# Softmax denominators of the graph units: inverted on 16 columns and spread by small transfers instead of VectorE transposes

## The chip, the cores and the metric

The kernel runs on one core of one Trainium2 chip. The metric is the time of one execution on the device, in microseconds (us); three runs of the kernel before took 3496.37, 3509.16 and 3542.75 us, so its median is 3509.16 us.

## The reference, cut to what matters

A sequence model of two layers. The first is an attention layer with 8 heads over 4 sequences of 1024 tokens of 128 numbers. The second is a graph of six nodes, each of them an attention layer without mask over the same tokens, whose query, key and value come from earlier nodes:

```python
for c in range(6):
    nsrc = min(c + 1, 5); snode = c - nsrc
    q = ew[c, 0] * (nodes[c - 1] @ We[eq] + be[eq])
    k = ew[c, 1] * (nodes[snode] @ We[ek] + be[ek])
    v = ew[c, 2] * (nodes[snode + nsrc // 2] @ We[ev] + be[ev])
    # mha: heads of 16; scores = qh @ kh.T / 4; attn = softmax(scores); ctx = attn @ vh; ctx @ Wo[c]
    nodes[c] = act_w[c] * mha(q, k, v, Wq[c], Wk[c], Wv[c], Wo[c]) + q
```

At the end stand a layer norm and the residual. Everything is float32. The change lies in the division by the softmax's sum, in the graph alone.

## The kernel before, in words

The graph (function `graph`) has 24 **units**, one for each node and sequence, in a fixed order; unit u + 4 reads what unit u stored in DRAM. A unit has 8 heads in two halves of 4 (`QUAD`), and 2 chunks of 512 queries. That makes 4 **groups** of a unit (`NG`; first both chunks of the first half, then both of the second) and 96 in the graph. Group g of the graph is group g % 4 of unit g // 4; "the unit's last group" is its fourth.

A unit is written as 46 **rounds** (the last unit, which prepares nothing for another, has 64). In a round PE makes the transposed scores of one head for 128 keys by 512 queries twice into one pair of PSUM banks (`pair`), and once more into the bank `psX` (a single). ACT takes the exponential of the pair in one instruction (L1454) and of the single in another (L1460). There is one pair bank, so the next round's pair waits for the exponential of this one. Some rounds use `psX` for something else: the next unit's values and projections, the transposed maxima (`turn`), or the unit's output. A table by the round's number sets this (`V_ROUND`, `PJ_ROUND`, `TURN_ROUND`, `OUT_ROUND`).

**Maxima.** The softmax needs each query's maximum beforehand. For the next unit PE computes all scores once more in 64 pieces of 128x1024 (`maxima`, L1262) into two PSUM buffers, and DVE reduces each piece (L1491). Piece p waits until piece p - 2 is reduced (`mx_done`). The pieces are spread over the rounds, about 1.4 a round.

**Contexts and denominators.** `contexts` multiplies the exponentials with the values of 4 heads at once, each head in a slot of 32 PSUM partitions: 16 rows of context and 16 equal rows of the sum of exponentials, since half the value columns are ones. When a group's 8 blocks of keys are done, ACT copies the 128x512 result to SBUF (`c_b`, L1439). Then DVE inverts the denominators in three steps, one in each of the three rounds after the copy, between reductions: a transpose of 32x32 blocks (`den_b`, L393), a reciprocal of the one column in 32 that holds a sum and a copy that spreads it over 16 columns (L403, L405), and a transpose back (`rec_b`, L414). GpSimd multiplies (`normalise`, L1552 and L1555), and for the second half adds the first (L1557). PE turns the chunk's context into the output (L1336, L1337), ACT copies it (`nt_b`, L1433), and SP stores it in DRAM.

**What sets the order.** Each engine's instructions are a list written out in Python; it executes them in that order and waits on semaphores. SP issues all transfers of the graph, and its list for a unit (`unit` in the block of SyncE) is: the second half of the stacked queries and keys of unit u + 1 (`stack`, 12 transfers `qs_`/`ks_<-partd`), the loads for its values and for the projection of unit u + 2 (`xq`, `xk`, `xv`), the rows of maxima (`maxima_rows`, 4 transfers `qs<-mpart` of 8 KB), the previous unit's second store, the residual's loads, the spill of unit u + 2 (`partd<-part`, 2 MB) and the first half of its stack, the next unit's rows of maxima, and the first store. On SP a wait for a semaphore keeps everything behind it waiting.

In the traces `_b` marks tiles of the graph, `ps_max` the maxima's buffers, `ps_pair` the pair bank, `ps_misc` psX.

Of the kernel before, what the change touches and what calls it, by code (L numbers as in the profile page):

```python
# [100 lines left out]
def program(nc, x, w_qk, w_v, w_out, b_out, conv, conv_rev, ew, act_w, We, be, Wq, Wk, Wv, Wo, ln_g, ln_b,  # L101
            ident, exchange, out):
    def dram(name, shape):
        return nc.dram_tensor(name, shape, F32, kind="Internal").ap()

    xnt = dram("xnt", [BATCH, P, TOK])
    x1d = dram("x1d", [BATCH * NCHUNK, P, BPC, DIM])
    node = dram("node", [UNITS + BATCH, P, TOK])
    ext = dram("ext", [4, HEADS, NE])
    wpd = dram("wpd", [NODES, P, WP_COLS])  # L110
    wvd = dram("wvd", [NODES, P, P])
    wfd = dram("wfd", [NODES, P, WF_COLS])
    partd = dram("partd", [P, 2, 2, TOK])
    x_rows = x.rearrange("b (t p) d -> b p t d", p=P)
    out_rows = out.rearrange("b (t p) d -> b p t d", p=P)

    with ExitStack() as ctx:
        def psum(name, n):
            return ctx.enter_context(nc.psum_tensor(name, [P, n], F32))

        psM = [psum(f"ps_max{i}", TOK) for i in range(2)]
        psP = psum("ps_pair", 2 * CHUNK)
        psS = [psP[:, CHUNK * i:CHUNK * i + CHUNK] for i in range(2)]
        psO = psum("ps_ctx", CHUNK)
        psX = psum("ps_misc", CHUNK)
        sid = ctx.enter_context(nc.sbuf_tensor("ident_sb", [P, P], F32))
# [8 lines left out]
        graph(nc, psM, psP, psO, psX, sid, wpd, wvd, wfd, node, partd, stored)  # L135
        finish(nc, psM, sid, node, x1d, ln_g, ln_b, out_rows)


# [859 lines left out]
    return slice(i, i + 1) if isinstance(i, int) else bass.ds(i, 1)  # L998


def graph(nc, psM, psP, psO, psX, sid, wpd, wvd, wfd, node, partd, stored):

    with ExitStack() as ctx:
# [14 lines left out]
        c32, rec = sb("c32_b", [P, 2, CHUNK]), sb("rec_b", [P, CHUNK])  # L1020
        den, inv = sb("den_b", [P, CHUNK]), sb("inv_b", [P, CHUNK // SLOT])
# [17 lines left out]
        o_copied, den_step, rec_ready, cn_done = sem("b_o_copied"), sem("b_den_step"), sem("b_rec_ready"), sem("b_cn_done")  # L1039
        fin_ready, fin_copied = sem("b_fin_ready"), sem("b_fin_copied")  # L1040

        PJ = 2 * NCHUNK
# [2 lines left out]
        NG = 2 * NCHUNK  # L1045
        STACK = 4 * len(TERMS) * D16
        MROWS = 4 * D16
        AHEAD = PIECES + 4
        LAST = UNITS - 1

        V_ROUND = {9: 0, 12: 1}
        PJ_ROUND = {14: 0, 18: 1, 20: 2, 23: 3}
        TURN_ROUND = ({33: 0, 16: 1}, {26: 0, 1: 1})
        OUT_ROUND = ({42: 0, 7: 1}, {58: 0, 10: 1})

        def single(u, r):

            turn = TURN_ROUND[u > 0].get(r)
            if turn == 1:
                return "turn", u, 1  # L1060
            if turn == 0 and u < LAST:
                return "turn", u + 1, 0
            out = OUT_ROUND[u == LAST].get(r)
            if out is not None and u >= out:
                return "output", u - out, out
# [65 lines left out]
        with nc.Block() as block:  # L1131
            @block.sync
            def _(sp):
# [47 lines left out]
                def maxima_rows(w, q):  # L1181
                    sp.wait_ge(mp_done, 2 * w + q + 1)
                    for k in range(2):
                        for odd in range(2):
# [45 lines left out]
                stack(1, 0)  # L1230
                for u in range(UNITS):
                    unit(u)
                store(LAST, 1)
                sp.wait_ge(stored, (UNITS + BATCH) * NCHUNK * D16)

# [251 lines left out]
            def _(dve):  # L1487
# [13 lines left out]
                def inverses(at):  # L1501

                    for step in range(1, 4):
                        g = GROUP_ROUND.get(at - step)
                        if g is None:
                            continue
                        if step == 1:
                            denominators_turned(nc, dve, c32, den, g, g % 2, o_copied, den_step, ones)
                        elif step == 2:
                            denominators_inverted(nc, dve, den, inv, wide, g // 2 % 2, g, cn_done, den_step)  # L1510
                        else:
                            inverses_turned(nc, dve, rec, wide, g // 2 % 2, g, rec_ready, den_step, ones)

                def unit(u):
                    for r in range(ROUNDS[u]):
                        for w, p in pieces_at(u, r, 0):
                            maxima(w, p)
                        inverses(sum(ROUNDS[:u]) + r)
                        for w, p in pieces_at(u, r, 1):
                            maxima(w, p)  # L1520

                nc.vector.memset(neg[:], -1.0).then_inc(minus, 1)
                for i in range(2):
                    nc.vector.memset(wide[i][:], 0.0)
                    for q in range(2):
                        ins = nc.vector.memset(vs[i][:, :, QUAD * q:QUAD * q + QUAD, DV * (1 - q):DV * (2 - q)], 1.0)
                ins.then_inc(ones, 1)
# [3 lines left out]
                    maxima(0, p)  # L1531
                for u in range(UNITS):
                    unit(u)
                g = NG * UNITS - 1
                denominators_turned(nc, dve, c32, den, g, 1, o_copied, den_step, ones)
                denominators_inverted(nc, dve, den, inv, wide, 1, g, cn_done, den_step)
                inverses_turned(nc, dve, rec, wide, 1, g, rec_ready, den_step, ones)

            @block.gpsimd
            def _(pool):  # L1540
# [3 lines left out]
                    nc.gpsimd.tensor_tensor(mpart[:, 1], m32[:], mpart[:, 0].bitcast(F32), ALU.subtract).then_inc(mp_done, 1)  # L1544

                def normalise(u, g):
                    pool.wait_ge(rec_ready, NG * u + g + 1)
                    if u:
                        pool.wait_ge(fin_ready, NCHUNK * (u - 1) + g % 2 + 1)
                    c = g % 2  # L1550
                    if g < 2:
                        nc.gpsimd.tensor_tensor(cn[:, 0, c], c32[:, c], rec[:], ALU.mult).then_inc(cn_done, 1)  # L1552
                        return

                    nc.gpsimd.tensor_tensor(cn[:, 1, c], c32[:, c], rec[:], ALU.mult).then_inc(cn_alone, 1)  # L1555
# [149 lines left out]
```

## Time and profile before

| | |
|---|---|
| median of three runs | 3509.16 us |
| profiled execution | 3483.55 us |
| its span, first to last instruction | 3481.7 us |
| TensorE busy (matmul) | 3058.8 us, 88% |
| VectorE busy | 2517.9 us, 72% |
| ScalarE busy | 2290.9 us, 66% |
| GpSimd busy | 489.1 us, 14% |
| mean granted TensorE clock | 0.953 of 2.4 GHz |

The preparation and the first attention layer take the first 950 us, the graph runs from there to about 3435 us, and the final layer norm ends the program. Busy shares are averages over these stages. "PEld" is the loading of weights into TensorE, "SPq" the issue of transfers on SP; an idle time in square brackets is what an engine stood idle just before an instruction, and behind the arrow is what released it. A transfer's time to landing runs from its issue to the semaphore.

### The profile page before, as it was taken

How to read it: one execution, taken by the hardware profiler on the slowest of the kernel's cores; microseconds unless marked ns; L12 is line 12 of the kernel's file. 1: busy time of each engine (PE TensorE's matmuls, PEld its weight loads, DVE VectorE, ACT ScalarE, POOL GpSimd, SP SyncE). 2: the span in 40 equal slices, each digit the busy share in tenths (PEclk: the TensorE clock that was granted, in tenths of full speed). 3: DMA queues.
4: the chain of work that ended last, by engine and by line, in shares of the span. 5: the costliest groups of instructions: out<-in, count | busy, mean ns of one | idle time of the engine just before them, and what ended most of it. 6: DMA issues, size and time to landing. Idle time of an engine off the chain costs nothing. (4 is left out here: it accounts for less than half of the span.)

```text
span 3481.7 us, 46771 instructions
## 1 busy us (share of the span) xinstructions
PE 3058.8 (88%) x17215; PEld 1373.0 (39%) x17215; DVE 2517.9 (72%) x2916; ACT 2290.9 (66%) x3238; POOL 489.1 (14%) x392
## 2 busy tenths in 40 slices
PE   5699998999758999999999999999999999999994
PEld 4466665656413333333333333333333333333331
DVE  5756554555248888888888788878888888888853
ACT  1355665655515677777777677777777777777783
POOL 0211101111000011111111111111111111111103
PEclk9899999999858999999999899999999999999996
DMA  5000000000144343344334433433444334433402
GB/s 162 16 10 4 23 1 20 7 10 10 36 100 95 67 96 68 79 89 96 85 65 96 87 66 85 93 91 67 87 96 96 67 78 90 96 83 66 82 15 80
DMA packets 100143, 231.38 MB, mean 66 GB/s; under 512 B 18162, under 2 KB 54534, under 8 KB 96838
## 3 DMA queue, kind: packets, MB, share of 16 engines
q1 hardware_dynamic: 99334, 226.23, 28.5%
q8 instruction: 140, 2.29, 0.3%
q10 hardware_dynamic: 576, 2.10, 0.2%
q14 instruction: 93, 0.76, 0.1%
HBM read 152.94 MB, written 73.34 MB: 65 GB/s over the span
## 5 line engine op out<-in xcount | busy, mean ns | idle before, releaser
L1491 DVE TENSOR_REDUCE mx_b<-ps_max 128x2 f32<-128x1024 f32 x1536 | 1814.3, 1217 | 416.3 <-PE ps_max L1262 414.5
L1454 ACT ACTIVATE pt_b<-ps_pair 128x1024 f32<-128x1024 f32 x1079 | 1106.1, 1025 | 490.1 <-PE ps_pair L1276 489.0
L1328 PE MATMUL ps_ctx<-pt_b,vs 128*32 128x512 f32 x6144 | 838.0, 618 | 4.6 <-ACT c_b L1439 4.0
L1262 PE MATMUL ps_max<-ks,qs 48*128 48x512 f32 x3072 | 746.9, 433 | 53.5 <-DVE mx_b L1491 27.2
L1276 PE MATMUL ps_pair<-qs,ks 50*128 50x512 f32 x2158 | 544.8, 501 | 171.9 <-ACT pt_b L1454 168.8
L1276 PEld LDWEIGHTS ps_pair<-qs,ks 50*128 50x128 f32 x2158 | 203.7, 186 | 935.3 <-ACT pt_b L1454 524.8
L766 ACT ACTIVATE pt<-ps_pair,cb 128x512 f32<-128x512 f32 x470 | 313.1, 687 | 310.3 <-PE ps_pair L623 226.8
L1460 ACT ACTIVATE pt_b<-ps_misc 128x512 f32<-128x512 f32 x830 | 491.9, 593 | 2.0 <-PE ps_misc L1276 0.5
L1262 PEld LDWEIGHTS ps_max<-ks,qs 48*128 48x128 f32 x3072 | 377.1, 192 | 217.9 <-DVE mx_b L1491 133.8
L819 DVE TENSOR_REDUCE mx<-ps_max 128x2 f32<-128x1024 f32 x256 | 303.5, 1221 | 150.6 <-PE ps_max L595 88.4
L1276 PE MATMUL ps_misc<-qs,ks 50*128 50x512 f32 x830 | 340.1, 410 | 3.1 <-ACT part L1407 0.9
L618 PE MATMUL ps_pair<-qhh,khl 128*128 128x512 f32 x470 | 233.0, 496 | 26.0 <-DMA qlm<-mhl 16.9
L1128 POOL TENSOR_TENSOR part<-full,part 128x512 fp32r<-128x512 f32 x92 | 117.9, 1281 | 919.9 <-ACT part L1407 919.9
L1328 PEld LDWEIGHTS ps_ctx<-pt_b,vs 128*32 128x32 f32 x6144 | 121.8, 108 | 276.4 <-issue 240.2
L592 PE MATMUL ps_max<-khl,qhh 128*128 128x512 f32 x512 | 193.5, 451 | 11.8 <-DVE mx L819 9.3
L1555 POOL TENSOR_TENSOR cn_b<-c_b,rec_b 128x512 f32<-128x512 f32 x48 | 61.5, 1281 | 946.6 <-DVE rec_b L414 946.6
L620 PE MATMUL ps_pair<-qlm,khm 96*128 96x512 f32 x470 | 189.8, 404 | 0.0
L1276 PEld LDWEIGHTS ps_misc<-qs,ks 50*128 50x128 f32 x830 | 157.5, 190 | 66.9 <-ACT pt_b L1460 30.3
L960 POOL TENSOR_SCALAR khm<-khl 64x512 fp32r<-64x512 f32 x64 | 94.8, 1486 | 388.8 <-PE ps_pair L620 248.6
L623 PE MATMUL ps_pair<-tab_scores,ident_sb 128*128 128x266 f32 (+2 forms) x588 | 138.6, 316 | 0.0
L635 PE MATMUL ps_ctx<-pt,vs 128*32 128x512 f32 x1024 | 137.9, 611 | 0.6 <-ACT c_a L755 0.6
L592 PEld LDWEIGHTS ps_max<-khl,qhh 128*128 128x128 f32 x512 | 91.4, 192 | 98.0 <-DVE mx L819 58.6
(151 smaller groups left out, 2420.3 us busy)
## 6 DMA issues: line engine op xcount, KB each, us to landing
partd<-part SPq DMA_DIRECT2D x24, 2048.0 KB, 6.4
qs<-partd SPq DMA_DIRECT2D x288, 128.0 KB, 5.7
ks<-partd SPq DMA_DIRECT2D x288, 128.0 KB, 6.7
xq<-node SPq DMA_DIRECT2D x24, 512.0 KB, 9.6
xk<-node SPq DMA_DIRECT2D x24, 512.0 KB, 10.5
xv<-node SPq DMA_DIRECT2D x24, 512.0 KB, 11.5
xf<-node SPq DMA_DIRECT2D x24, 512.0 KB, 4.2
node<-nt_b SPq DMA_DIRECT2D x48, 256.0 KB, 2.0
```

Source lines behind the costliest of these rows:

```text
L592: ins = pe.matmul(psM[p % 2][:, CHUNK * kc:CHUNK * kc + CHUNK], qhh[q][:, i, P * qb:P * qb + P], khl[q][:, i, CHUNK * kc:CHUNK * kc + CHUN ...
L618: pe.matmul(bank, khl[q][:, i, P * kb:P * kb + P], qhh[q][:, i, CHUNK * qc:CHUNK * qc + CHUNK], start=True, stop=False)
L620: ins = pe.matmul(bank, khm[:, i, P * kb:P * kb + P], qlm[q][:, i, CHUNK * qc:CHUNK * qc + CHUNK], start=False, stop=hi == 0)
L623: ins = pe.matmul(bank[:, lo:hi], sid[:], tabS[:, sd_, QUAD * q + i, at:at + hi - lo], start=False, stop=True)
L766: act.activation(pt[:, s % 2, i], score_bank(psS, psM, n, last), ACT.Exp, scale=SCALE_A, bias=cb[:, QUAD * q + i, at:at + 1]).then_inc(exp ...
L819: nc.vector.tensor_reduce(mx2[:, p], psM[p % 2][:].rearrange("p (c n) -> p c n", c=NCHUNK), AX.X, ALU.max).then_inc(mx_done, 1)
L1262: ins = pe.matmul(psM[p % 2][:, CHUNK * odd:CHUNK * odd + CHUNK], qs[w % 2][rows, 2 * q + j, P * qb:P * qb + P], ks[w % 2][rows, 2 * q + j ...
L1276: return pe.matmul(bank, ks[u % 2][rows, h // 2, P * kb:P * kb + P], qs[u % 2][rows, h // 2, CHUNK * qc:CHUNK * qc + CHUNK], start=True, s ...
L1328: ins = pe.matmul(psO[SLOT * i:SLOT * i + SLOT, :], vs[u % 2][:, kb, QUAD * (s // HALF_STEPS) + i], pt[:, entry(u, QUAD * s + i)], start=k ...
L1454: act.activation(pt[:, at:at + 2].rearrange("p k n -> p (k n)"), pair_bank(u, r)[:], ACT.Exp, scale=SCALE_B).then_inc(exp_done, 1)
L1460: act.activation(pt[:, entry(u, k)], psX[:], ACT.Exp, scale=SCALE_B).then_inc(exp_done, 1)
L1491: nc.vector.tensor_reduce(mx2[:, kc, q, :, KB * j + qb], psM[p % 2][:].rearrange("p (h n) -> p h n", h=2), AX.X, ALU.max).then_inc(mx_done, 1)
```

## The change

The first 92 groups (all of units 0 to 22) no longer use DVE's transposes. SP now issues, for each group (`denominators`):

1. four transfers that lay one head's row of 512 sums out over 32 partitions, 16 numbers on each (`den_b<-c_b`), after which DVE inverts 128x16 numbers (`inverse`);
2. one transfer of these inverses to DRAM (`invd`);
3. four that read a head's row of 512 inverses from there and write it to 16 partitions (`rec_b<-invd`).

DVE's `inverse(g)` stands three rounds after the group's copy, where the second transpose stood. `rec` has two buffers now. The last unit's four groups keep the transposes (`inverse_here`), all steps together. The outputs of a unit stood in its round 42 and in round 7 of the next; now both stand in the next unit's rounds 4 and 10, and both stores are issued there. The rows of maxima of a unit's second half are split on GpSimd before the previous unit's last normalisation instead of after it.

```diff
-        OUT_ROUND = ({42: 0, 7: 1}, {58: 0, 10: 1})
+        OUT_ROUND = {4: 0, 10: 1}
...
+                def denominators(g):
+
+                    sp.wait_ge(o_copied, g + 1)
+                    for i in range(QUAD):
+                        at = SLOT * i + DV * (1 - g // NCHUNK % 2)
+                        sp.dma_start(den[SLOT * i:SLOT * i + SLOT],
+                                     c32[at:at + 1, g % 2].rearrange("o (p j) -> o p j", p=SLOT)).then_inc(den_in, D16)
+                    sp.wait_ge(inverted, g + 1)
+                    if g:
+                        sp.wait_ge(rec_in, REC * g)
+                    sp.dma_start(invd.rearrange("i (p j) -> (i p) j", p=SLOT), inv[:]).then_inc(inv_out, D16)
+                    sp.wait_ge(inv_out, D16 * (g + 1))
+                    if g:
+                        sp.wait_ge(cn_done, g)
+                    q = g // NCHUNK % 2
+                    for i in range(QUAD):
+                        at = SLOT * i + DV * q
+                        sp.dma_start(rec[q][at:at + DV], invd[i:i + 1].to_broadcast([DV, CHUNK])).then_inc(rec_in, D16)
...
                     if u < LAST:
                         load_values(u + 1)
-                    maxima_rows(u, 1)
                     if u:
+                        maxima_rows(u, 1)
+                        denominators(NG * u - 1)
+                        store(u - 1, 0)
                         store(u - 1, 1)
                     load_residual(u)
+                    if u < LAST:
+                        denominators(NG * u)
+                    if not u:
+                        maxima_rows(u, 1)
+                    if u < LAST:
+                        denominators(NG * u + 1)
                     if u < LAST - 1:
                         spill(u + 2)
                         stack(u + 2, 0)
                     if u < LAST:
                         maxima_rows(u + 1, 0)
-                    store(u, 0)
+                        denominators(NG * u + 2)
...
+                def inverse(g):
+
+                    dve.wait_ge(den_in, REC * (g + 1))
+                    if g:
+                        dve.wait_ge(inv_out, D16 * g)
+                    nc.vector.reciprocal(inv[:], den[:]).then_inc(inverted, 1)
...
-                        inverses(sum(ROUNDS[:u]) + r)
+                        g = GROUP_ROUND.get(sum(ROUNDS[:u]) + r - 3)
+                        if g is not None and g < NG * LAST:
+                            inverse(g)
...
                 def unit(u):
                     if u:
+                        split_maxima(u, 1)
                         normalise(u - 1, NG - 1)
-                        split_maxima(u, 1)
```

What this moves is seen best in two lists. First SP's, from the rows of maxima of a unit's second half to the spill, in the kernel before:

```order
L1144 DMA wp<-wpd 128x258
L1145 DMA xq<-node 128x1024
L1146 DMA xk<-node 128x1024
L1153 DMA wv_b<-wvd 128x128
L1154 DMA xv<-node 128x1024
L1188 DMA qs<-mpart 1x16x128 x4
L1194 DMA node<-nt_b 128x512
L1159 DMA wf<-wfd 128x257
L1160 DMA xf<-node 128x1024
L1165 DMA partd<-part 128x4096
```

And in the changed one:

```order
L1160 DMA wv_b<-wvd 128x128
L1161 DMA xv<-node 128x1024
L1195 DMA qs<-mpart 1x16x128 x4
L1202 DMA den_b<-c_b 32x1x16 x4
L1207 DMA invd<-inv_b 128x16
L1214 DMA rec_b<-invd 16x512 x4
L1220 DMA node<-nt_b 128x512 x2
L1166 DMA wf<-wfd 128x257
L1167 DMA xf<-node 128x1024
```

The nine transfers of the previous unit's last group come behind the stack, the loads and the rows of maxima; those of the unit's first and second group follow the residual's loads, and only then comes the spill, which waited for nothing of the kind before. The third group's stand behind the first half of the stack and the next rows of maxima.

Then DVE's list at the start of a unit, before (L1497 ends the maxima of the half before it):

```order
L1497 TENSOR_TENSOR mx_b<-mx_b 128x32
L1491 TENSOR_REDUCE mx_b<-ps_max 128x2 x3
L393 STREAM_TRANSPOSE den_b<-c_b 128x512
L1491 TENSOR_REDUCE mx_b<-ps_max 128x2
L403 RECIPROCAL inv_b<-den_b 128x16
L405 COPY wide_b<-inv_b 128x16x16
L1491 TENSOR_REDUCE mx_b<-ps_max 128x2 x2
L414 STREAM_TRANSPOSE rec_b<-wide_b 128x512
```

and now:

```order
L1532 TENSOR_TENSOR mx_b<-mx_b 128x32
L1526 TENSOR_REDUCE mx_b<-ps_max 128x2 x4
L1541 RECIPROCAL inv_b<-den_b 128x16
L1526 TENSOR_REDUCE mx_b<-ps_max 128x2 x18
L1541 RECIPROCAL inv_b<-den_b 128x16
```

Four reductions into the unit stands the reciprocal of the previous unit's last group, with a wait for its four layout transfers, and all later reductions are behind it.

## Rows read from the trace of the kernel before

**Rows 1.** Windows of the graph: microseconds, busy time of each engine, granted clock, DMA share.
```profile
1895.00:2005.60 110.60, 102.92 (x548) 37.72 (x546) 82.63 (x82) 74.94 (x104) 13.59 (x12) 0.86 0.34 76
2202.00:2300.00 98.00, 89.74 (x550) 33.53 (x548) 82.04 (x82) 74.92 (x104) 13.60 (x12) 1.00 0.38 85
```

**Rows 2.** Waits in 21 units: total us, times, longest.
```profile
PEld ps_max L1262 <- DVE mx_b L1491: 75.0, 164, 0.9
```

**Rows 3.** Groups of VectorE instructions: busy us, mean ns of one, idle before them.
```profile
L1491 DVE TENSOR_REDUCE mx_b<-ps_max 128x2 f32<-128x1024 f32 x1536 | 1814.3, 1217 | 416.3 <-PE ps_max L1262 414.5
L393 DVE STREAM_TRANSPOSE den_b<-c_b 128x512 f32<-128x512 f32 x96 | 67.6, 705 | 68.3 <-ACT c_b L1439 68.3
L414 DVE STREAM_TRANSPOSE rec_b<-wide_b 128x512 f32<-128x512 f32 x96 | 67.4, 702 | 0.5
L405 DVE COPY wide_b<-inv_b 128x256 f32<-128x256 f32 x96 | 28.3, 294 | 3.3
L403 DVE RECIPROCAL inv_b<-den_b 128x16 f32<-128x16 f32 x96 | 22.5, 235 | 0.5
```

**Rows 4.** Timeline of ACT, a unit's start: start us, duration us, instruction.
```profile
2280.33 0.60 ACT L1439 ACTIVATE c_b<-ps_ctx 128x512 f32<-128x512 f32 x1
```

**Rows 5.** Timeline of SP, the same unit's start.
```profile
2278.29 0.78 SPq L1178 DMA_DIRECT2D qs<-partd  x2
...
2286.17 0.43 SPq L1154 DMA_DIRECT2D xv<-node  x1
2289.32 2.40 SPq L1188 DMA_DIRECT2D qs<-mpart  x4
```

**Rows 6.** Transfers issued there, at 2284.3 to 2286.6: count, KB each, us to landing.
```profile
xv<-node SPq DMA_DIRECT2D x1, 512.0 KB, 10.8
```

**Rows 7.** The rows of maxima issued there, qs<-mpart, four transfers.
```profile
DMA to landing us min/median/max: 6.2/6.6/6.9
```

**Rows 8.** The same transfers with nothing else in flight, before unit 0.
```profile
DMA to landing us min/median/max: 1.8/1.8/1.9
```

**Rows 9.** Timeline of DVE, then of PE, at the same unit's start.
```profile
2285.47 0.70 DVE L414 STREAM_TRANSPOSE rec_b<-wide_b 128x512 f32<-128x512 f32 x1
...
2287.93 0.40 PE L1262 MATMUL ps_max<-ks,qs 48*128 48x512 f32 x2
```

**Rows 10.** Transfers, from the page: KB each, median us to landing.
```profile
node<-nt_b SPq DMA_DIRECT2D x48, 256.0 KB, 2.0
```

**Rows 11.** Windows around a wait of PE before unit 0.
```profile
1074.00:1076.00 2.00, 0.00 (x0) 0.00 (x0) 0.13 (x1) 0.00 (x0) 0.00 (x0) 1.00 1.04 397
...
1078.00:1080.00 2.00, 2.00 (x10) 1.77 (x12) 0.00 (x0) 0.08 (x1) 0.00 (x0) 0.50 0.00 0
...
1090.00:1092.00 2.00, 2.00 (x14) 1.74 (x13) 1.57 (x3) 0.82 (x3) 0.00 (x0) 0.71 0.00 0
```

**Rows 12.** Timelines of ACT, DVE and PEld in that unit.
```profile
2235.55 0.60 ACT L1439 ACTIVATE c_b<-ps_ctx 128x512 f32<-128x512 f32 x1
...
2241.81 0.70 DVE L414 STREAM_TRANSPOSE rec_b<-wide_b 128x512 f32<-128x512 f32 x1
...
2262.81 0.70 DVE L414 STREAM_TRANSPOSE rec_b<-wide_b 128x512 f32<-128x512 f32 x1
...
2266.59 0.19 PEld L1276 LDWEIGHTS ps_pair<-qs,ks 50*128 50x128 f32 x2 [0.60 <-ACT pt_b L1454]
```

**Rows 13.** Timeline of SP in the middle of the unit before.
```profile
2234.85 0.32 SPq L1165 DMA_DIRECT2D partd<-part  x1
2241.40 0.79 SPq L1178 DMA_DIRECT2D qs<-partd  x2
...
2246.90 2.40 SPq L1188 DMA_DIRECT2D qs<-mpart  x4
```

**Rows 14.** Timelines of ACT and PE, last unit.
```profile
3363.15 0.59 ACT L1439 ACTIVATE c_b<-ps_ctx 128x512 f32<-128x512 f32 x1
...
3369.86 0.59 PE L1337 MATMUL ps_misc<-cn_b,wf 128*128 128x512 f32 x1
```

More of the change, by code:

```diff
@@ L113, in program @@
     partd = dram("partd", [P, 2, 2, TOK])
+    invd = dram("invd", [QUAD, CHUNK])
     x_rows = x.rearrange("b (t p) d -> b p t d", p=P)
@@ L134, in program @@
                             tabS, tabM, stored)
-        graph(nc, psM, psP, psO, psX, sid, wpd, wvd, wfd, node, partd, stored)
+        graph(nc, psM, psP, psO, psX, sid, wpd, wvd, wfd, node, partd, invd, stored)
         finish(nc, psM, sid, node, x1d, ln_g, ln_b, out_rows)
@@ L998, in one, with graph @@
     return slice(i, i + 1) if isinstance(i, int) else bass.ds(i, 1)
-def graph(nc, psM, psP, psO, psX, sid, wpd, wvd, wfd, node, partd, stored):
+def graph(nc, psM, psP, psO, psX, sid, wpd, wvd, wfd, node, partd, invd, stored):
     with ExitStack() as ctx:
@@ L1019, in graph @@
         mpart = sb("mpart", [PIECES, 2, P], F32R)
-        c32, rec = sb("c32_b", [P, 2, CHUNK]), sb("rec_b", [P, CHUNK])
-        den, inv = sb("den_b", [P, CHUNK]), sb("inv_b", [P, CHUNK // SLOT])
+        c32 = sb("c32_b", [P, 2, CHUNK])
+        rec = [sb(f"rec_b{q}", [P, CHUNK]) for q in range(2)]
+        den, inv = sb("den_b", [P, CHUNK // SLOT]), sb("inv_b", [P, CHUNK // SLOT])
+        dent = sb("dent_b", [P, CHUNK])
         wide = [sb(f"wide_b{q}", [P, CHUNK // SLOT, SLOT]) for q in range(2)]
@@ L1038, in graph @@
         cn_alone = sem("b_cn_alone")
-        o_copied, den_step, rec_ready, cn_done = sem("b_o_copied"), sem("b_den_step"), sem("b_rec_ready"), sem("b_cn_done")
+        o_copied, cn_done = sem("b_o_copied"), sem("b_cn_done")
+        den_in, inverted, inv_out, rec_in = sem("b_den_in"), sem("b_inverted"), sem("b_inv_out"), sem("b_rec_in")
+        den_step, rec_ready = sem("b_den_step"), sem("b_rec_ready")
         fin_ready, fin_copied = sem("b_fin_ready"), sem("b_fin_copied")
@@ L1047, in graph @@
         MROWS = 4 * D16
+        REC = QUAD * D16
         AHEAD = PIECES + 4
@@ L1062, in single @@
                 return "turn", u + 1, 0
-            out = OUT_ROUND[u == LAST].get(r)
-            if out is not None and u >= out:
-                return "output", u - out, out
+            if r in OUT_ROUND:
+                return ("output" if u else "none"), u - 1, OUT_ROUND[r]
+            if u == LAST and r == 58:
+                return "output", u, 0
             if r in V_ROUND and u < LAST:
@@ L1232, in _ @@
                     unit(u)
+                store(LAST, 0)
                 store(LAST, 1)
@@ L1499, in maxima, with inverse_here @@
                                                 mx2[:, 1, q].rearrange("p h n -> p (h n)"), ALU.max).then_inc(mx_final, 1)
[L1501 to L1512, printed above, removed]
+                def inverse(g):
[3 more added lines that the diff above has]
+                    nc.vector.reciprocal(inv[:], den[:]).then_inc(inverted, 1)
+                def inverse_here(g):
+                    k, q = g - NG * LAST, g // NCHUNK % 2
+                    dve.wait_ge(o_copied, g + 1)
+                    nc.vector.transpose(dent[:], c32[:, g % 2]).then_inc(den_step, 1)
+                    dve.wait_ge(den_step, 3 * k + 1)
+                    dve.wait_ge(cn_done, g)
+                    if not k:
+                        dve.wait_ge(inv_out, D16 * g)
+                    nc.vector.reciprocal(inv[:], dent[:].rearrange("p (k r) -> p k r", r=SLOT)[:, :, DV * (1 - q)]
+                                         ).then_inc(den_step, 1)
+                    dve.wait_ge(den_step, 3 * k + 2)
+                    nc.vector.tensor_copy(wide[q][:, :, DV * q:DV * q + DV],
+                                          inv[:].unsqueeze(2).to_broadcast([P, CHUNK // SLOT, DV])).then_inc(den_step, 1)
+                    dve.wait_ge(den_step, 3 * k + 3)
+                    nc.vector.transpose(rec[q][:], wide[q][:].rearrange("p k r -> p (k r)")).then_inc(rec_ready, 1)
                 def unit(u):
@@ L1517, in unit @@
                             maxima(w, p)
-                        inverses(sum(ROUNDS[:u]) + r)
+                        g = GROUP_ROUND.get(sum(ROUNDS[:u]) + r - 3)
+                        if g is not None and g < NG * LAST:
+                            inverse(g)
+                        g = GROUP_ROUND.get(sum(ROUNDS[:u]) + r)
+                        if g is not None and g >= NG * LAST:
+                            inverse_here(g)
                         for w, p in pieces_at(u, r, 1):
@@ L1524, in _ @@
                     nc.vector.memset(wide[i][:], 0.0)
+                    nc.vector.memset(rec[i][:], 0.0)
                     for q in range(2):
@@ L1533, in _ @@
                     unit(u)
[L1534 to L1537, printed above, removed]
+                inverse_here(NG * UNITS - 1)
             @block.gpsimd
@@ L1546, in normalise @@
                 def normalise(u, g):
-                    pool.wait_ge(rec_ready, NG * u + g + 1)
+                    if u < LAST:
+                        pool.wait_ge(rec_in, REC * (NG * u + g + 1))
+                    else:
+                        pool.wait_ge(rec_ready, g + 1)
                     if u:
@@ L1551, in normalise @@
                     if g < 2:
-                        nc.gpsimd.tensor_tensor(cn[:, 0, c], c32[:, c], rec[:], ALU.mult).then_inc(cn_done, 1)
+                        nc.gpsimd.tensor_tensor(cn[:, 0, c], c32[:, c], rec[g // 2][:], ALU.mult).then_inc(cn_done, 1)
                         return
-                    nc.gpsimd.tensor_tensor(cn[:, 1, c], c32[:, c], rec[:], ALU.mult).then_inc(cn_alone, 1)
+                    nc.gpsimd.tensor_tensor(cn[:, 1, c], c32[:, c], rec[g // 2][:], ALU.mult).then_inc(cn_alone, 1)
                     pool.wait_ge(cn_alone, NCHUNK * u + c + 1)
```

## The prediction, made before the changed kernel was run

> **What bounds the kernel now.** I read the windows of the graph first. Unit 11 takes 98.00 us, and PE is busy for 89.74 of them, DVE for 82.04, ACT for 74.92 [rows 1]. PE is closest to full, so I asked next what PE waits for that the change touches. That is the maxima's buffers: in the 21 units from 1200 to 3300 us its weight loads waited 75.0 us for DVE's reductions, 3.6 us a unit [rows 2]. In all the graph DVE itself stood idle 416.3 us, nearly all of it waiting for PE's next piece [rows 3]. So DVE is not the bound. It is a partner of PE at a distance of two pieces: what keeps DVE for less than about two pieces costs nothing, what keeps it longer stops PE, and with PE the pairs and the exponentials.
>
> **What DVE gives up.** A group loses two transposes and the spreading copy, 0.705 + 0.702 + 0.294 = 1.70 us, and keeps the reciprocal of 0.235 us [rows 3]; over 92 groups that is 156 us. PE feels only what it waited for. The most is 3.6 us a unit, for 23 units 82 us. Reductions that follow each other closely make PE wait too, so not all of it is the transposes'; I take two thirds, an estimate: 2.4 us a unit, **-55 us**, and -82 to 0 as the ends.
>
> **The unit's last group, where I expect the loss.** I follow one unit, whose start lies near 2278 us; the others repeat it. The denominators are copied at 2280.33 and ready at 2280.9 [rows 4]. The layout transfers cannot start then. SP issues the stack from 2278.29 on, then the loads, the last of them at 2286.17 [rows 5], together 8.3 us. The rows of maxima come next. Before, they waited for GpSimd until 2289.32; their split now precedes the normalisation, so they go at 2286.6 and take 2.40 us [rows 5], until 2289.05. Only then come the four layout transfers. Their issue is bounded by 0.43 us each (a plain load) and 0.60 (a row of maxima, also small pieces) [rows 5]; they resemble the latter, so they are issued at 2291.45.
>
> Nor do they land soon. Of the loads before them the last is issued at 2286.17 and lands 10.8 us later, at 2297.0 [rows 6]. The rows of maxima, 8 KB each, take 6.2 to 6.9 us in this place and end near 2297.4 [rows 7]; the same four took 1.8 us with nothing else in flight [rows 8]. Small transfers thus share the lot of what was issued ahead. I put the layout's landing at 2298.0, the two ends being 2293.2 (issue plus 1.8) and 2298.5.
>
> DVE meets this wait in round 3, just before the place where the second transpose started at 2285.47 [rows 9]. It still owes PE piece 4 of the unit. PE may write pieces 4 and 5, and stops before piece 6, which it began at 2287.93 before [rows 9]. It goes on when the layout has landed, the reciprocal (0.24) and the reduction of piece 4 (1.22) are through [rows 3]: at 2299.45. PE is stopped 11.5 us, in units 1 to 22, **+253 us**; with the early landing 6.7 us, +147.
>
> One rule of the Trainium skill speaks of the same transfers: "DMA: Bandwidth & Descriptors", section "Anatomy of one DMA — SWDGE (gpsimd) path", gives a transfer a fixed part of about 2 us and the rest by its bytes. It is written for transfers that GpSimd issues; taken over to SP's 8 KB ones, it agrees with the 1.8 us of the empty queue [rows 8] and not with 6.2 to 6.9 in the busy one [rows 7]. By it the stop would be the early landing's, +147 us instead of +253.
>
> The rest of that group's chain is hidden. From 2298.2: issue and landing of the inverses 0.4 + 2.0 us (a store to DRAM) [rows 10], four reads back at 0.43 and 1.8 to land, GpSimd's two passes about 2.6, so 2306.8. The output that needs it stands in round 10, and PE is in round 5 at 2299.5; five rounds of 98/46 = 2.1 us bring it there at 2310.
>
> **The clock.** Before unit 0 PE stood idle between 1074 and 1078 us; the granted clock was 1.00 at 1074, 0.50 (1.2 GHz) from 1078 on, and still changing back between 1090 and 1092 [rows 11], so 13 us at the lower level. A unit with 31 us at that level ((1 - 0.86) x 110.6 / 0.5) took 110.6 us instead of 98.0 [rows 1]: 0.41 us lost for each. The new stop is longer than that idle time. If the clock falls in it and stays low for 10 us of work, a unit loses 4 us: **+88 us** in 22 units, from 0 to 22 x 5.3 = 117.
>
> **First group of a unit.** SP has nothing in hand then, and the queue is empty. From the copy's end: four issues 2.4, landing 1.8, together 4.3 us. DVE's place is three rounds after, 5.6 us in the one traced next (copy's end 2236.15, transpose 2241.81 [rows 12]). Nothing is added, at worst 1 us.
>
> **Second group, and through it the third.** Copies move one round later, as round 4 no longer makes a single: the copy ends at 2238.0 instead of 2236.15 [rows 12], the layout lands at 2242.3, DVE is there at 2243.7, hidden. But SP stays with this group: inverses issued and landed 2246.4, reads back issued until 2248.1. The spill, at 2234.85 before [rows 13], is 13.2 us late, and with it the stack (2241.40 before) and the rows of maxima (until 2249.3) [rows 13]. These have slack, since the next unit starts near 2278. What is late next is the third group's layout: issued from 2262.5 to 2264.9, behind the stack in a full queue; the rows ahead of them, last issued at 2261.9 and taking about 7 us as in [rows 7], end near 2268.9, and the layout at 2269.3. DVE waits for it from round 39, near 2264.7 (the transpose of round 38 was at 2262.81 [rows 12]); PE stops in round 40, whose pair loads at 2266.59 [rows 12], near 2267.3, and resumes at 2270.8. **+77 us** (22 x 3.5), from 0 to 22 x 6.
>
> **The last unit** has its clock off: a copy ended at 3363.7, and its output followed at 3369.9 [rows 14]. By way of SP the chain takes about 13 us from the copy, more if the rows of maxima go first: **+8 us** once. Moving outputs and stores adds no work. Unit u + 4 needs the node two units after it is stored.
>
> **The sum.** -55 + 253 + 88 + 77 + 8 = +371. The profiled execution took 3483.55 us, giving 3855; it lies 26 us under the median of 3509.16. I say **3850 us**.
>
> **Rivals.**
> 1. *The small transfers overtake.* They land 1.8 us after their issue even behind the loads. The last group's stop is 6.7 us (+147), the third group's 1.4 (+31), with the last unit's 8 and -55: +131, 3615 us, and up to 3700 if the clock falls too. For it: a transfer of 64-byte pieces might use engines that are free. Against it: the rows of maxima did not [rows 7]. 0.13.
> 2. *Faster: the wait on DVE is covered.* If the layout is in SBUF when DVE comes to its reciprocal, the price is only the gain: 55 to 82 us less, 3400 to 3430. It decides at 2287.93, the piece PE needs: the layout would have to land by 2286.5, 2.6 us before SP, by rows 5, starts to issue it. Against it stand five us at least. 0.02 for faster by over 2%, 0.05 for no change, where parts of it meet smaller stops.
> 3. *PE never warms again.* If the stop in each unit keeps the clock low for 40 us of work, 0.41 x 40 x 22 = 361 us in place of 88, near 4130. Against it: 13 us sufficed in rows 11. 0.08.
> 4. *The change does nothing to the end*, because PE is the bound and its work is the same. The stops above are stops of PE; its 0.03 is part of the 0.05 of rival 2.
>
> **How the numbers follow.** My case has 0.72; its range is 3720 to 3960. The overall range, 3600 to 3980, takes in the first rival. From the runs shown, about 2% is what can be told from no change: faster by more 0.02, within 0.05, slower 0.93.
>
> **What would show it.** In the changed kernel's profile DVE's reciprocal should have long idle time before it, released by `den_b<-c_b`, some 12 us once a unit and 4 to 5 once more, and next to none for the first two groups. `den_b<-c_b` should land in 2 us for these and in about 7 for the others. PE's matmuls of L1297, the maxima, should wait for DVE by some 15 us a unit, windows behind that should show a clock of 0.50, and a unit should take 114 us. The spill should be issued 13 us later in its unit. If a layout transfer behind the loads lands in 2 us, the first rival holds; if the reciprocal waits for nothing, the second.

## The result and the profile after

The changed kernel takes 3996.05 us (median of 4 runs, 3987.79 to 4013.93), the kernel before 3502.76 us beside it. The ratio is 1.143 (95% interval 1.137 to 1.150): 493 us slower. The forecast was slower, 3850 us, in a range of 3600 to 3980; the measured time lies 16 us above the range. All times and ratios here are of undisturbed executions; the one trace of the experiment `filled` is of a disturbed one (9781 us) and is not read.

From the page after: busy time and share of each engine, the granted clock in 40 slices, then two groups (busy us, mean ns, idle time before them and its releaser):

```profile
PE 3291.2 (82%) x17215; PEld 1444.7 (36%) x17215; DVE 2396.4 (60%) x2642; ACT 2286.2 (57%) x3238; POOL 487.7 (12%) x392
...
PEclk9999999996699887888877888878887888978897
...
L1297 PE MATMUL ps_max<-ks,qs 48*128 48x512 f32 x3072 | 825.3, 473 | 366.5 <-DVE mx_b L1526 343.6
...
L1541 DVE RECIPROCAL inv_b<-den_b 128x16 f32<-128x16 f32 x92 | 22.8, 248 | 402.3 <-DMA den_b<-c_b 402.3
```

From the page of the kernel before:

```profile
PEclk9899999999858999999999899999999999999996
...
L1262 PE MATMUL ps_max<-ks,qs 48*128 48x512 f32 x3072 | 746.9, 433 | 53.5 <-DVE mx_b L1491 27.2
```

VectorE is busy for 121 us less; the removed instructions summed up to 156, by durations that partly overlap [rows 3]. What grew is idle time: 402.3 us before the reciprocals, waiting for the layout transfers, and 343.6 us before TensorE's maxima, waiting for VectorE (27.2 before the change). And the clock, 9 and more in most slices of the graph before, stands at 7 and 8 in most of them now.

The waits from 1200 to 3900 us (total us, times, longest):

```profile
DVE inv_b L1541 <- DMA den_b<-c_b: 388.8, 43, 14.4
...
PEld ps_max L1297 <- DVE mx_b L1526: 375.8, 109, 12.1
...
PE ps_max L1297 <- DVE mx_b L1526: 316.7, 43, 11.8
```

Two waits a unit, as forecast, and TensorE's own share of them is 316.7 us. One more stop, of 10.5 us, stands just before 1200. Taken one by one from TensorE's timeline, the last group's 22 stops sum to 220 us, 10.0 each (2.5 to 11.8), and the third group's 21 to 107 us, 5.1 each: 327 us in all, 14.9 a unit (the forecast had 253 and 77, 11.5 and 3.5 each). I follow one unit; its first stop is the longest of the 22. Its start, on VectorE:

```profile
2405.33 2.36 DVE L1526 TENSOR_REDUCE mx_b<-ps_max 128x2 f32<-128x1024 f32 x2 [0.48 <-PE ps_max L1297]
2422.07 0.25 DVE L1541 RECIPROCAL inv_b<-den_b 128x16 f32<-128x16 f32 x1 [14.38 <-DMA den_b<-c_b]
```

This answers to the transpose in [rows 9]: the reciprocal of the last group stands behind four reductions and waits 14.38 us. SP's part, from the same unit's start to the third group:

```profile
2400.94 0.78 SPq L1185 DMA_DIRECT2D qs<-partd  x2
...
2408.71 0.43 SPq L1161 DMA_DIRECT2D xv<-node  x1
2409.19 2.44 SPq L1195 DMA_DIRECT2D qs<-mpart  x4
2411.67 2.50 SPq L1202 DMA_DIRECT2D den_b<-c_b  x4
...
2484.16 0.42 SPq L1172 DMA_DIRECT2D partd<-part  x1
2491.82 0.78 SPq L1185 DMA_DIRECT2D qs<-partd  x2
...
2497.32 2.44 SPq L1195 DMA_DIRECT2D qs<-mpart  x4
2499.80 2.48 SPq L1202 DMA_DIRECT2D den_b<-c_b  x4
```

Compare with [rows 5] and [rows 13]. Stack and loads take 8.2 us, the rows of maxima follow at once, and the layout goes out from 2411.67 on, 10.7 us after the stack's start. Its landing, beside the last of the rows of maxima (count, KB each, us to landing):

```profile
den_b<-c_b SPq DMA_DIRECT2D x4, 2.0 KB, 7.9
qs<-mpart SPq DMA_DIRECT2D x1, 8.0 KB, 10.3
```

A transfer of 2 KB takes 7.9 us here. On TensorE the stop between the pair of round 5 and the next piece of maxima is in the brackets:

```profile
2411.15 0.50 PE L1311 MATMUL ps_pair<-qs,ks 50*128 50x512 f32 x2
2423.46 0.79 PE L1297 MATMUL ps_max<-ks,qs 48*128 48x512 f32 x2 [11.81 <-DVE mx_b L1526]
```

11.81 us; 11.5 were forecast, and the mean is 10.0. The other three reciprocals of the unit:

```profile
2454.11 0.24 DVE L1541 RECIPROCAL inv_b<-den_b 128x16 f32<-128x16 f32 x1
...
2480.71 0.24 DVE L1541 RECIPROCAL inv_b<-den_b 128x16 f32<-128x16 f32 x1
...
2507.96 0.25 DVE L1541 RECIPROCAL inv_b<-den_b 128x16 f32<-128x16 f32 x1 [6.57 <-DMA den_b<-c_b]
```

The first and second group wait for nothing, the third waits 6.57 us: its layout is issued at 2499.80, behind the late spill (2484.16), the stack and the rows of maxima.

Now the clock. Windows of 4 us (busy TensorE with its count, weights, VectorE, ScalarE, GpSimd; then granted clock, DMA share, GB/s), at the first stop and at the second:

```profile
2412.00:2416.00 4.00, 0.00 (x0) 0.00 (x0) 0.00 (x0) 0.86 (x1) 0.00 (x0) 1.00 1.03 247
...
2420.00:2424.00 4.00, 0.54 (x2) 0.50 (x3) 1.93 (x3) 0.00 (x0) 0.00 (x0) 0.50 0.03 4
...
2428.00:2432.00 4.00, 4.00 (x17) 1.46 (x16) 1.35 (x2) 2.00 (x3) 1.60 (x2) 0.50 0.00 0
2432.00:2436.00 4.00, 4.00 (x16) 0.98 (x13) 3.46 (x3) 2.54 (x4) 0.00 (x0) 0.50 0.00 0
2436.00:2440.00 4.00, 4.00 (x29) 1.98 (x25) 1.23 (x1) 1.80 (x4) 0.00 (x0) 0.86 0.00 0
2440.00:2444.00 4.00, 4.00 (x21) 1.45 (x19) 2.82 (x3) 2.88 (x4) 0.00 (x0) 1.00 0.12 44
...
2508.00:2512.00 4.00, 2.65 (x12) 0.56 (x12) 3.55 (x4) 0.00 (x0) 0.00 (x0) 0.50 0.10 27
...
2520.00:2524.00 4.00, 4.00 (x18) 1.15 (x14) 3.58 (x3) 2.74 (x4) 0.00 (x0) 0.50 0.00 0
2524.00:2528.00 4.00, 4.00 (x24) 1.80 (x20) 2.41 (x3) 1.80 (x3) 0.00 (x0) 0.77 0.02 7
2528.00:2532.00 4.00, 3.24 (x25) 1.39 (x28) 3.09 (x4) 3.65 (x7) 0.45 (x1) 1.00 1.10 166
```

The first stop ends at 2423.5; the clock is 0.50 (1.2 GHz) in the window from 2420 on, and the 0.86 of the window from 2436 means that it came back near 2437.1, 13.6 us after the stop's end. The second stop ends at 2509.3, and the clock is back near 2525.8 (0.77 in the window from 2524), 16.5 us later. In all windows of 4 us between 1300 and 3800 the clock was low for 789 us in 40 separate falls, about two a unit of some 20 us each. Part of that is the stop itself: in windows of 1 us, TensorE was at work for 601 of the 789 us, 15 a fall and 28 a unit (a unit takes 117 us now). In the low windows with TensorE at work for at least half of the window (130 of them) ScalarE was busy for 1.61 us in four, against 3.12 in the 374 at full clock: about half the speed of progress. Before, between 1300 and 3300 us, the low time was 58 us.

### The profile page after: what moved, and what is told of

Read it like the earlier page. It is cut to its first block and busy times, and to the rows that moved or that the text cites. A ratio compares the mean times of both kernels' runs of the same rounds, so it can differ in the third digit from the quotient of the medians.

```text
span 3990.5 us, 47294 instructions
## 1 busy us (share of the span) xinstructions
PE 3291.2 (82%) x17215; PEld 1444.7 (36%) x17215; DVE 2396.4 (60%) x2642; ACT 2286.2 (57%) x3238; POOL 487.7 (12%) x392
## 5 line engine op out<-in xcount | busy, mean ns | idle before, releaser
L1297 PE MATMUL ps_max<-ks,qs 48*128 48x512 f32 x3072 | 825.3, 473 | 366.5 <-DVE mx_b L1526 343.6
L1363 PE MATMUL ps_ctx<-pt_b,vs 128*32 128x512 f32 x6144 | 950.7, 695 | 3.5 <-ACT c_b L1474 3.0
L1311 PE MATMUL ps_pair<-qs,ks 50*128 50x512 f32 x2158 | 584.9, 538 | 127.9 <-ACT pt_b L1489 125.0
L1297 PEld LDWEIGHTS ps_max<-ks,qs 48*128 48x128 f32 x3072 | 420.4, 214 | 522.9 <-DVE mx_b L1526 436.2
L1311 PEld LDWEIGHTS ps_pair<-qs,ks 50*128 50x128 f32 x2158 | 219.2, 200 | 998.5 <-ACT pt_b L1489 397.1
L1311 PE MATMUL ps_misc<-qs,ks 50*128 50x512 f32 x830 | 382.2, 461 | 11.8 <-ACT part L1442 10.1
L1541 DVE RECIPROCAL inv_b<-den_b 128x16 f32<-128x16 f32 x92 | 22.8, 248 | 402.3 <-DMA den_b<-c_b 402.3
L1311 PEld LDWEIGHTS ps_misc<-qs,ks 50*128 50x128 f32 x830 | 178.4, 215 | 106.2 <-ACT pt_b L1495 43.8
## 6 DMA issues: line engine op xcount, KB each, us to landing
xk<-node SPq DMA_DIRECT2D x24, 512.0 KB, 10.5
```

What stands on the lines that cost most here:

```text
L1297: ins = pe.matmul(psM[p % 2][:, CHUNK * odd:CHUNK * odd + CHUNK], qs[w % 2][rows, 2 * q + j, P * qb:P * qb + P], ks[w % 2][rows, 2 * q + j ...
L1311: return pe.matmul(bank, ks[u % 2][rows, h // 2, P * kb:P * kb + P], qs[u % 2][rows, h // 2, CHUNK * qc:CHUNK * qc + CHUNK], start=True, s ...
L1363: ins = pe.matmul(psO[SLOT * i:SLOT * i + SLOT, :], vs[u % 2][:, kb, QUAD * (s // HALF_STEPS) + i], pt[:, entry(u, QUAD * s + i)], start=k ...
```

## The experiments

There are three groups of experiments: which of the transfers cost the time, whether VectorE's place in the order decides it, and what the clock's share is. The kernel before ran beside each batch, with medians of 3488 to 3499 us. Experiments are compared by their medians; those of before in the four batches and beside the changed kernel differ by 15 us.

### One group at a time

In all four the outputs, stores and maxima have their new places, and `by_dma` says which groups of a unit go by transfers; the others keep the three steps of before on VectorE.

```diff
+        BY_DMA = ()        # none_by_dma;  (0, 1) first_two;  (2,) third_only;  (3,) last_only
+        def by_dma(g):
+            return g < NG * LAST and g % NG in BY_DMA
...
```

**none_by_dma.** 

> The changed kernel with its outputs, stores and maxima in their new places, but all groups back on VectorE's transposes, in three steps as before. Theory A (TensorE is stopped where VectorE waits for a late layout transfer, and its clock falls in the stop): about the time of before, 3480 to 3520 us. Rival B (each group sent over SP costs the same, some 5.3 us, by traffic and SP's time): also 3500. Rival C (the moved outputs and stores cost the time): near 3990.

Measured: 3522 us, ratio 1.0075 (1.0043 to 1.0107). The moved outputs cost 24 us, not the loss. What in them costs that is not settled; in the traces, from 1300 to 3300 us, TensorE waits 24.7 us for the reductions (before 7.3) and the clock is low for 106 us (before 58).

**first_two.** 

> Only the first and second group of each unit go by transfers, the third and the last are transposed as before. A: their layout is in time, no stop, and half of the transposes are gone: 3460 to 3490 us, a gain of about 1 us a unit. B: half of the loss, near 3750.

Measured: 3502 us, ratio 1.0007 (0.9968 to 1.0047); 20 us less than none_by_dma and 12 above A's upper end. No reciprocal waits. The gain over before is not there; that the moved outputs took it is argued from none_by_dma and not shown. Rival B is out by 248 us.

**third_only.** 

> Only the third group of each unit goes by transfers. A: with the second group off SP the spill and the stack are on time, so the third group's layout is no longer late: 3480 to 3510 us, VectorE's reciprocal idle under 1 us. If this group's stop came from its own place and not from the late spill: a stop of about 5 us and a slow clock behind it, 3700. B: a quarter of the loss, near 3625.

Measured: 3460 us, ratio 0.9883 (0.9832 to 0.9934). Faster than before, and 20 us below A's lower end. It is 62 us under none_by_dma, though the steps taken off VectorE sum to 39 us at most (23 x 1.70). The traces differ in the clock too: it was low for 41 us here from 1300 to 3300 us, against 106. Whether that makes the rest was not tested.

**last_only.** 

> Only the last group of each unit goes by transfers, laid out behind the loads and the rows of maxima of the next unit. A: the stop of about 10 us in each of 22 units stays, and with it some 13 us of work at a granted clock of 0.50, together 15 to 17 us a unit: 3830 to 3880 us. B: a quarter of the loss, near 3625.

Measured: 3881 us, ratio 1.1086 (1.1034 to 1.1138). The last group alone makes 359 us over none_by_dma, 16.3 us a unit, three quarters of the whole loss. TensorE's waits for the reductions from 1200 to 3700 us, 22 units:

```profile
PE ps_max L1307 <- DVE mx_b L1536: 259.0, 65, 11.8
```

11.8 us a unit (its 22 long stops alone sum to 233 us, 10.6 each); with what comes on top, the slow clock by the section below, it makes 16.3.

### The second group's hold on SP

```diff
-        BY_DMA = (2,)
+        BY_DMA = (1, 2)
```

**second_third.** 

> The second and the third group by transfers, the others transposed. A: the second group's chain holds SP, the spill comes 13 us late, and the third group's layout with it: against third_only (3460) a stop and a slow clock come back, about 9 us a unit, 3650 us, with the spill late in the trace. If the spill's delay does not matter: 3460.

Measured: 3690 us, ratio 1.0541 (1.0485 to 1.0597), 231 us over third_only and 40 more than expected. SP's times in one unit, second group's layout, spill, third group's layout:

```profile
2436.77 2.44 SPq L1211 DMA_DIRECT2D den_b<-c_b  x4
...
2445.20 0.42 SPq L1179 DMA_DIRECT2D partd<-part  x1
...
2460.35 2.49 SPq L1211 DMA_DIRECT2D den_b<-c_b  x4
```

and in third_only, spill and layout:

```profile
2423.26 0.32 SPq L1179 DMA_DIRECT2D partd<-part  x1
...
2448.06 2.44 SPq L1211 DMA_DIRECT2D den_b<-c_b  x4
```

From the spill to the layout it is 15.2 us in second_third and 24.8 in third_only: there the spill goes early and the stack has left the queue when the layout comes; here the layout follows right behind the stack. What the reciprocals waited for it in all, second_third and then third_only:

```profile
  DMA den_b<-c_b: 115.5, 22
```

```profile
  DMA den_b<-c_b: 2.1, 4
```

So the third group's stop is made by the second group's chain, as the prediction had it; stop and slow clock together cost 10.5 us a unit, where 9 were expected.

### VectorE later

`later` keeps every transfer of the changed kernel; only VectorE looks for the result later. The output that needs the last group moves with it, and SP lays out the first group before it waits for that output.

```diff
-        OUT_ROUND = {4: 0, 10: 1}
+        OUT_ROUND = {4: 0, 17: 1}
+        LAG = (3, 3, 6, 10)        # rounds from a group's copy to its reciprocal, 3 before
...
                         store(u - 1, 0)
-                        store(u - 1, 1)
-                    load_residual(u)
                     if u < LAST:
                         denominators(NG * u)
+                    if u:
+                        store(u - 1, 1)
+                    load_residual(u)
```

**later.** 

> All groups by transfers as in the changed kernel, but VectorE's reciprocal stands 10 rounds after the last group's copy and 6 after the third's (3 before), and the second output in round 17 instead of 10. A: transfers land as late as before, but VectorE comes later still: no stop, all of the transposes saved: 3420 to 3480 us. B: the traffic and SP's time stay: 3990.

Measured: 3441 us, ratio 0.9827 (0.9775 to 0.9878). It beats both kernels: 555 us under the changed one and 58 under the kernel before beside it, a gain of 1.2 to 2.2% by the interval. The reciprocals, and the window from 1300 to 3300 us:

```profile
L1543 DVE RECIPROCAL inv_b<-den_b x92: 241/244/253, 1090.8 to 3322.6; 128x16 f32<-128x16 f32 x92
...
  DMA den_b<-c_b: 8.4, 1
```

```profile
1300.00:3300.00 2000.00, 1822.92 (x11189) 684.90 (x11189) 1588.35 (x1436) 1526.69 (x2127) 274.71 (x242) 1.00 0.41 90
```

One wait in 92 reciprocals. The clock is 1.00 in this stretch, with no fall in it.

**later_but_third** has LAG = (3, 3, 3, 10). 

> As later (3441 us), but the third group's reciprocal back at 3 rounds after the copy, behind the late spill. The stop of some 5.5 us comes back with one fall of the clock: 230 us more, as between third_only and second_third, 3650 to 3680. If the clock falls only once a unit and the last group's stop had it to itself in the changed kernel, the third's stop would cost 5 us a unit here: 3560.

Measured: 3704 us, ratio 1.0620 (1.0552 to 1.0688), 263 us over `later`, 12 a unit. The first theory holds, with 24 us more than its upper end: the third stop has its own fall of the clock (19 falls in 2100 us of the trace, one for each of these waits):

```profile
PE ps_max L1299 <- DVE mx_b L1528: 97.8, 19, 6.3
```

The stops are 5.1 us each; some 6.8 us a unit of the 12 come on top of them, with one fall of the clock a unit.

**last_lag7** and **last_lag10** send the last group alone, with LAG 7 and 10 for it and the output in round 17. 

> Only the last group by transfers (as last_only, 16.3 us a unit slower than none_by_dma), but VectorE's reciprocal 7 rounds after the copy instead of 3 and the second output in round 17. Some four rounds of the stop, 8 us, are gone and 2 to 4 us of it stay. If a stop costs only its own length: 3522 + 22 x 3 = 3590. If each stop also costs a fall of the clock whatever its length, some 6 us more a unit: 3690 to 3730.

> The same with the reciprocal 10 rounds after the copy: no stop and no fall of the clock in either theory; a quarter of the transposes saved against none_by_dma: 3490 to 3520 us.

Measured: 3607 us, ratio 1.0342 (1.0282 to 1.0401), and 3511 us, ratio 1.0045 (1.0013 to 1.0077). The waits of last_lag7 from 1300 to 3400 us, some 20 units:

```profile
PE ps_max L1309 <- DVE mx_b L1538: 65.2, 39, 4.0
```

3.3 us of stop a unit cost 96 us in all, 4.4 a unit. The second theory, a full fall for each stop, is wrong at this length: the clock was low for 147 us in 22 mostly short falls, against 505 us in the same stretch of last_only.

**layout_first** sends only the last group's layout ahead of the stack; VectorE's places are as in the changed kernel.

```diff
+                    if u:
+                        lay_out(NG * u - 1)
                     if u < LAST:
                         stack(u + 1, 1)
```

> The changed kernel with the last group's four layout transfers issued ahead of the next unit's stack and loads; the rest of its chain stays behind them. A: they land 2 us after issue, VectorE no longer waits there, and 16 us a unit come back; the stack and loads start some 5 us later, which may stop TensorE at the values of round 9 or the output of round 10 for up to 5 us: 3640 to 3750 us, the third group's stop unchanged. B (traffic): unchanged, 3990.

Measured: 3906 us, ratio 1.1141 (1.1080 to 1.1202), 156 us more than the upper end. TensorE's waits in it, 1200 to 3800 us:

```profile
PE ps_max L1304 <- DVE mx_b L1533: 101.3, 22, 6.6
PE ps_misc L1292 <- DMA xv<-node: 100.8, 21, 7.0
PE ps_misc L1378 <- POOL cn_b L1616: 48.0, 22, 4.0
```

The last group's wait on VectorE is gone; what is left on the maxima is the third group's. In its place TensorE waits 4.8 us a unit for the values' load (L1292), which now starts late, and 2.2 for the normalised context (L1378). I had counted these stops without the fall of the clock behind them; it was low for 635 us of the 2400 from 1300 on. Shorter stops in more places bought little.

### The clock's share

**filled** puts matmuls into the two stops, which change nothing else.

```diff
+                        if 0 < u < LAST and r in (5, 40):
+                            single_free(*last_single(u, r))
+                            for _ in range(40 if r == 5 else 16):
+                                score(u, FIRST[u][r], psX[:])
```

> The changed kernel with matrix work in TensorE's two stops of units 1 to 22: 40 matmuls of a score into psX at the start of round 5 and 16 at the start of round 40, each overwritten by the next and never read. The stops of VectorE stay. Theory A, clock part: the granted clock stays at 1.00 behind the stops, and if some 30 us of work a unit at 0.50 cost 0.41 us each, 12 us a unit come back: 3700 to 3780 us. If the clock costs only the 4 us a unit of the prediction: near 3910. If the lost time is the stops alone: 3990 or more.

Measured: 4118 us, ratio 1.1746 (1.1678 to 1.1814), and a mean clock of 0.85 in its timed runs, against 0.86 in the changed kernel. The filling did not hold the clock, and the kernel lost 5.5 us a unit more. By its time alone this would be the third case of the expectation, the stops alone; but the condition of the test, a clock kept up, was not met, so it decides nothing. Without a trace, why is open.

**filled_wide** takes products over all 128 rows: `pe.matmul(psX[:, 0:P], sid[:], sid[:], start=True, stop=True)`, 70 and 35 times. 

> As filled, but the matrix work in the two stops uses all 128 rows of the array and is short: 70 products of the 128x128 identity with itself at the start of round 5, 35 at the start of round 40 (eight products of that size took 1.16 us in the trace of before), never read. Theory A, clock part: the clock stays at 1.00 behind the stops and 10 to 15 us a unit come back, 3670 to 3780 us. If the clock stays up and the time does not fall, the clock was no part of the loss; if it falls all the same, nothing is decided.

Measured: 3968 us, ratio 1.1366 (1.1302 to 1.1429). Windows at the first stop, in the filling, at its end, and behind:

```profile
2398.00:2402.00 4.00, 4.00 (x38) 4.00 (x37) 0.00 (x0) 0.00 (x0) 0.00 (x0) 1.00 0.55 188
...
2406.00:2410.00 4.00, 4.00 (x36) 3.83 (x36) 0.00 (x0) 0.00 (x0) 2.33 (x2) 1.00 0.27 82
...
2414.00:2418.00 4.00, 3.53 (x24) 1.23 (x21) 3.61 (x4) 3.21 (x5) 0.00 (x0) 1.00 0.02 4
```

The clock stays at 1.00, in all windows from 1300 to 3700 us. The time fell by only 28 us, and missed the expected range by 188. The reason is the filling's length: 105 products took 22.3 us a unit, 7.4 more than the stops, and TensorE no longer waited for VectorE at all. I had taken the length from eight records of 1.16 us, but the trace has two records for each product (4620 here for 2310), so those eight were four products. So this run gives back and spends about the same: 28 + 22 x 7.4 = 191 us, 8.7 a unit, for the clock (an estimate).

**filled_fit** has 48 and 20 products. 

> As filled_wide, with the filling cut to the length of the two stops: in filled_wide 105 products took 22.3 us a unit (0.21 us each) against stops of 14.6 us, so what the clock gave back was spent again. Here 48 and 20 products, 10.2 and 4.3 us. Theory A with the clock's share read from the runs so far (3996 - 3441 - 8 = 547 us, 24.9 a unit, less 14.6 of stops: 10 us a unit): the clock stays at 1.00 and the time falls to 3770 to 3810 us. If the clock's share is the 4 us a unit of the prediction: 3900 to 3920.

Measured: 3832 us, ratio 1.0980 (1.0916 to 1.1044), 164 us under the changed kernel. The stops stay: VectorE waited 421.3 us for the layouts from 1200 to 3700 us, 402.3 in the whole of the changed kernel. TensorE's remaining wait for the reductions, and the window from 1300 to 3400 us:

```profile
PE ps_max L1297 <- DVE mx_b L1530: 32.0, 41, 8.5
```

```profile
1300.00:3400.00 2100.00, 1952.11 (x12560) 907.13 (x12559) 1404.93 (x1284) 1370.38 (x1907) 247.68 (x219) 0.99 0.36 79
```

With the clock at 0.99 instead of 0.84 the same stops cost 7.5 us a unit less. That is a lower bound of the clock's share, since the filling overlaps the stops only roughly (1.5 us a unit of waiting was left). The time lies between my two expectations, 22 us above the nearer.

## Why the prediction was right in direction and missed the range

- **Which engine is the bound** held as far as the runs go. `later`, which has VectorE's relief and no stop, is 58 us faster than the kernel before beside it; I took 55 of at most 82. That this is all relief is not shown: from 1300 to 3300 us the clock is low for 58 us before and never in `later`, which at 0.41 us each would be some 24 us of it.
- **The last group's layout** held in each step: issue 10.7 us after the stack's start (forecast 10.8), landing 7.9 us after issue (6.5), TensorE stopped 11.81 us (11.5). Over all units the stops are shorter, 10.0 us on average and 220 us in all, where 253 were forecast. last_only shows that it makes most of the loss.
- **The chain from the second group to the third** held in kind: the spill is late, the third layout lands late, and second_third brings the stop back. Its size was a little more: VectorE waited 6.57 us (4.6), and TensorE 5.1 (107 us in 21 units; 5.1 again in later_but_third) where I said 3.5, 77 in all. Both stops together were 330 us in the forecast and are 327 in the trace: that the sum fits so well is luck, since 33 us too many at the one meet 30 too few at the other.
- **The first two groups** are free, as said.
- **The last unit** waited 6.9 us once, 8 forecast:

```profile
PE ps_misc L1371 <- POOL cn_b L1609: 6.9, 1, 6.9
```

- **The clock** is the term that failed: the mechanism was right, its size was not. I gave it 4 us a unit, +88 in all, with 117 as its upper end: one fall a unit, 10 us of slow work at 0.41 us lost for each. The trace has two falls a unit, since the third group's stop brings one too, though the prediction named that stop itself, and each leaves 13 to 19 us of slow work in most units, 28 us a unit together. filled_fit measures at least 164 us for it, 7.5 a unit. The balance of the medians allows at most 221, 10.0 a unit: 3996 = 3441 (`later`, no stop) + 327 + 7 + the rest. Some 30 us of this rest are neither stop nor slow clock: with the clock kept up, filled_wide is still 29 us over 3441 + 22 x 22.3 + 7, and filled_fit 32 over 3441 + 22 x (14.5 + 1.5) + 7. So I estimate the clock's share at 190 us, and what the 30 are is open.
- **The loss for each us of slow clock** was not too low in the forecast. 28 us of slow work at 0.41 would be 253 us in 22 units, more than the balance leaves, and ScalarE's busy time (half the progress) overstates it further. What I had wrong is how long and how often, not how much for each.
- **The base and the range.** The sum of +371 was put on the profiled execution of 3483.55 us, 19 under the median of 3502.76 that it is held against; the same sum on the median gives 3874. The upper ends of the terms, 0 + 253 + 117 + 132 + 8, reach 3994 even so, and the range stopped at 3980.
- **Rival 1** (small transfers overtake) is refuted by the landing of 7.9 us; on an empty queue the same four took 2.3. **Rival 2** (the wait is covered) was wrong of this kernel, and `later` shows what it took: 7 more rounds for the last group and 3 for the third. **Rival 3** (TensorE does not warm again) had the low time of a unit nearly right, 40 us against 37 (789 us in 2500), though not for its reason: the clock comes back, but falls twice. It priced these 40 us at 361, and the balance allows 221.

## What to carry to other kernels

In this kernel a transfer of 2 KB landed 2.3 us after its issue on an empty queue and 7.9 us behind a stack and loads, and its issue came 10.7 us late by the issuing engine's list. So replace work on an engine by transfers only with the consumer moved behind their real landing. A wait placed in a busy engine's list holds all that stands behind it there, and whoever waits for that; here seven and three rounds more of distance turned a loss of 14% into a gain of 1.7%. And when a forecast contains a stop of TensorE, price the slow clock behind it for each stop, not once: here stops of 5 us and of 10 us each had their own fall, while stops of 3.3 us cost little beyond themselves.

## What the hardware showed that I had not expected

- A stop of 4 to 12 us was followed by some 15 us of work at 1.2 GHz (601 us in 40 falls; 13.6 and 16.5 in the unit shown), though TensorE was busy without a gap in the windows shown. ScalarE's busy time in these stretches was 1.61 / 3.12 = 52% of that at full clock. Stops of 3.3 us (last_lag7) left only some 7 us of low clock a unit.
- Matmuls whose result nobody reads, put into a stop, kept the clock at 1.00 in filled_wide and at 0.99 in filled_fit; in filled the mean was 0.85, about as without any, and why is open. In this kernel they are no gain, only a way to measure.
- The write of the inverses to DRAM landed in 1.4 us and the four reads back in 1.8 (medians); 2.0 and 1.8 had been taken for them from stores and rows of maxima.
